# Distance attention: the position products written to PSUM in one row without gaps, and ACT's copies reading them with a stride

## The chip, the cores and the metric

The kernel runs on one core of a Trainium2 chip. The metric is the device time of one execution in microseconds (us). The times given for the kernel before are those of three executions, with their median.

## The reference

The model is a chain of layers over x of shape (8, 512, 128), all float32: a wave attention, a mixture of experts, a distance attention, and the same mixture of experts again, each after a layer norm and added to x. Only the distance attention is touched:

```python
# B = 8, S = 512, 16 heads of 8 dims, hidden 128
q = (x @ Wq.T + bq).reshape(B, S, HEADS, HEAD_DIM)      # k and v alike
scores = jnp.einsum('bqhd,bkhd->bhqk', q, k) / math.sqrt(HEAD_DIM)
pos_emb = dist_emb[MAX_POS - 1 + distance]              # distance = pos_q - pos_k
scores = scores + jnp.einsum('bqhd,qkd->bhqk', q, pos_emb)
scores = scores + jnp.einsum('bkhd,qkd->bhqk', k, pos_emb)
probs = jax.nn.softmax(scores, axis=-1)
ctx = jnp.einsum('bhqk,bkhd->bqhd', probs, v)
```

The second and the third line of scores are the two parts that the change is about: for a query position and a key position both take the same row of a table of distances, once against q and once against k.

## The kernel before, in words

**Sizes.** P = 128 is a tile of positions, QT = 4 tiles make the 512 positions, BH = 32 is the number of (batch, head) pairs worked at a time (two batches of 16 heads). The float32 operands are split into bfloat16 parts beforehand, 48 rows of them, and laid at rows 0 and 64 of a tile, so that a product reads 112 rows.

**Units and groups.** The function `distance_attention` walks NU = 64 units. A unit u is one pair of a query tile q and a key tile kt for 32 heads, with q, kt = divmod(u, 4). Four units (kt = 0 to 3) make a group, that is one query tile against all keys; there are 16 groups. In the text a unit is named by its kt, and "unit 0 of the next group" follows unit 3.

**Steps of a unit.** The order on TensorE (PE) is written out by hand in `unit_steps` and `plan`:

- "r", eight times (CH = 8): `positions` (L1690) computes the position products of 16 places for 32 heads, for the query part and the key part (s = 2) at once. It issues 8 products (HALF = 8). Each takes one slice of the table T, 128 columns wide, as its weights, and one pair of places of qk as the data that moves: 2 parts x 2 places x 32 heads = 128 columns. The 8 products fill a slot of psR (two PSUM banks of 512 float32). ACT's `keep` (L1772) copies the slot to r in SBUF, where a head's 128 places lie together. r has one buffer, so the first copy of a unit waits for VectorE (DVE) to have finished with the unit before.
- "c", four times: `content` (L1707) computes q times k for 8 heads (L1714) and adds to it the query part turned by a transpose of r (L1717). DVE's `add` (L1807, the instruction is L1814) adds the key part and writes S. Content begins when ACT has done all eight copies.
- With the fourth unit of a group S is complete. Then, during unit 0 of the next group, DVE takes the maxima and subtracts them (`maximum`, L1822 to L1829), PE turns S ("e", `turn`, L1726), ACT takes the exponential (`weigh`, L1786), PE multiplies with the values ("pv", `values`, L1742), ACT copies the result (L1794) and PE turns it ("o", L1751). In that unit six of the eight r steps stand ahead of the first e, the other two after e steps 1 and 3, and the four c steps near the end.

All steps but pv take a slot of psR in turn. There are RING = 3 slots, so a step waits until the step three before it has been read.

**What feeds a unit.** SP loads the parts of k for unit u (`load_k`, L1615) once the content of unit u - 2 is done. POOL (GpSimd) then spreads them to qk (`spread_k`, two copies at L1653), and the first r step of the unit waits for that. After the spread of unit 2 of a group POOL also spreads the next group's q (`spread_q`, two copies more), ahead of the spread of unit 3.

**The lines of the change.** In `positions` the output of a product is a view in which a part's 32 heads are 8 elements apart and its 2 places lie side by side:

```python
out = slot[:, 2 * j // HALF, :].rearrange("p (s h n) -> p s n h", s=2, h=BH)
mm = pe.matmul(out[:, :, n:n + 2, :], T[:, w:w + P], qk[...], start=(n == 0), stop=True, ...)
```

The product writes it in the order part, place, head, so that each of its 128 results goes 8 elements (32 bytes) behind the one before. The slot then holds, per bank, 64 (part, head) pairs with 8 places side by side, and ACT reads each bank from end to end, writing to r in runs of 8.

**Elsewhere**, a line that the rows name: in the wave output DVE's L977 reads from PSUM one column of each 32, four bytes every 128 bytes.

Of the kernel before, what the change touches and what calls it, by code (L numbers as in the profile page):

```python
# [15 lines left out]
P = 128  # L16
# [1494 lines left out]
def distance_attention(nc, sb, ps, sem, a, X, ident, dram):  # L1511
# [8 lines left out]
    BH = NB * H  # L1520
# [4 lines left out]
    CP = P // CH  # L1525
    HALF = CP // 2
    HB = BH // 4
    NPAIR = BH // 2
    RING = 3
# [35 lines left out]
    with ExitStack() as c:  # L1565
        T = sb(c, "T", [ROWS, WIN], BF16)
        qs = sb(c, "qs", [ROWS, 2, BH, P], BF16)
        ks = sb(c, "ks", [ROWS, 2, BH, P], BF16)
        qk = sb(c, "qk", [ROWS, 4, PAIRS, 2, BH], BF16)
        r = sb(c, "r", [P, 2, BH, P])  # L1570
# [4 lines left out]
        m = sb(c, "m", [P, BH])  # L1575
# [3 lines left out]
        psR = ps(c, "psR", [P, RING, 2, L])  # L1579
# [11 lines left out]
        act_took = sem(c, "act_took")  # L1591
# [86 lines left out]
        @block.tensor  # L1678
        def _(pe):

            def free_slot(n):
                if n >= RING:
                    old = fills[n - RING]
                    if old in by_act:
                        pe.wait_ge(act_took, by_act[old])
                    else:
                        pe.wait_ge(dve_took, by_dve[old])
                return psR[:, n % RING, :, :]

            def positions(u, k):  # L1690
                q, kt = divmod(u, QT)
                mine, theirs = q % 2, 2 + u % 2
                w0 = L - 1 + P * (kt - q % QT) - (P - 1)
                if k == 0:
                    pe.wait_ge(qb_ready, 2 * (q + 1))
                    pe.wait_ge(kb_ready, 2 * (u + 1))
                slot = free_slot(fill["r", u, k])
                for j in range(HALF):
                    pair = k * HALF + j
                    w, n = w0 + 2 * pair, 2 * j % HALF  # L1700
                    out = slot[:, 2 * j // HALF, :].rearrange("p (s h n) -> p s n h", s=2, h=BH)
                    mm = pe.matmul(out[:, :, n:n + 2, :], T[:, w:w + P],  # L1702
                                   qk[:, mine:theirs + 1:theirs - mine, pair, :, :], start=(n == 0), stop=True,
                                   skip_group_check=True)
                mm.then_inc(filled, 1)

            def content(u, k):  # L1707
                q = u // QT
                if k == 0:
                    pe.wait_ge(act_took, by_act["r", u, CH - 1])  # L1710
                slot = free_slot(fill["c", u, k]).rearrange("p a (h n) -> p (a h) n", n=P)
                for j in range(HB):
                    h = k * HB + j
                    pe.matmul(slot[:, j, :], qs[:, q % 2, h, :], ks[:, u % 2, h, :], start=(j % HG == 0),  # L1714
                              stop=False, skip_group_check=True)
                for j in range(HB):
                    mm = pe.matmul(slot[:, j, :], r[:, 0, k * HB + j, :], ident[:], start=False, stop=True,  # L1717
                                   is_transpose=True, skip_group_check=True)
                mm.then_inc(filled, 1)

            def turn(q, j):
                pe.wait_ge(shifted, q * BH + 2 * j + 2)
                slot = free_slot(fill["e", q, j])
                for i in range(2):
                    for kt in range(QT):
                        mm = pe.matmul(slot[:, i, kt * P:(kt + 1) * P], S[:, 2 * j + i, kt * P:(kt + 1) * P],  # L1726
                                       ident[:], start=(kt == 0), stop=True, is_transpose=True,
                                       skip_group_check=True)
                mm.then_inc(filled, 1)

            def values(q, j):
                i, g = divmod(j, GPB)
                pe.wait_ge(act_took, by_act["e", q, 2 * j + 1])
                if g == 0:
                    if i == 0:
                        pe.wait_ge(v_loaded, 16 * NB * (q // QT + 1))
                    if q:
                        pe.wait_ge(o_taken, (q - 1) * NB + i + 1)
                for kt in range(QT):
                    for h in range(HG):  # L1740
                        row, pair = h * (P // HG), q * NPAIR + 2 * j + h // 2
                        mm = pe.matmul(psO[row:row + VW, i, g, :], Vb[:, i, g, kt, h, :],  # L1742
                                       W[:, pair % RING_W, h % 2, kt * P:(kt + 1) * P],
                                       start=(kt == 0), stop=(kt == QT - 1), skip_group_check=True)
                mm.then_inc(pv, 1)

            def outputs(q, i):
                pe.wait_ge(o_taken, q * NB + i + 1)
                slot = free_slot(fill["o", q, i])
                for g in range(GPB):  # L1750
                    mm = pe.transpose(slot[:, 0, g * P:(g + 1) * P], oS[:, g * P:(g + 1) * P], ident[:])  # L1751
                mm.then_inc(filled, 1)

            pe.wait_ge(t_loaded, 32)
            pe.wait_ge(zeroed, 2)
            pe.wait_ge(psO_clear, 1)
            for kind, i, k in plan:
                if kind == "r":
                    positions(i, k)
                elif kind == "c":  # L1760
                    content(i, k)
                elif kind == "e":
                    turn(i, k)
                elif kind == "pv":
                    values(i, k)
                else:
                    outputs(i, k)

        @block.scalar
        def _(act):  # L1770

            def keep(u, k):  # L1772
                n = fill["r", u, k]
                act.wait_ge(filled, n + 1)
                if u:
                    act.wait_ge(dve_took, by_dve["c", u - 1, 3])
                act.copy(r[:, :, :, k * CP:(k + 1) * CP].rearrange("p s h (a n) -> p a (s h) n", a=2),  # L1777
                         psR[:, n % RING, :, :].rearrange("p a (m n) -> p a m n", n=HALF)).then_inc(act_took, 1)

            def weigh(q, j):  # L1780
                n = fill["e", q, j]
                act.wait_ge(filled, n + 1)
                pair = q * NPAIR + j
                if pair >= RING_W:
                    act.wait_ge(pv, (pair - RING_W) // 2 + 1)
                act.activation(W[:, pair % RING_W, :, :].rearrange("p a n -> p (a n)"),  # L1786
                               psR[:, n % RING, :, :].rearrange("p a n -> p (a n)"),
                               ACT.Exp, scale=1.0 / SHARP).then_inc(act_took, 1)

            def take(q, i):  # L1790
                if q or i:
                    act.wait_ge(filled, fill["o", q - (i == 0), 1 - i] + 1)
                act.wait_ge(pv, q * NQUAD + (i + 1) * GPB)
                act.copy(oS[:].rearrange("p (g n) -> p g n", g=GPB), psO[:, i, :, ::-1]).then_inc(o_taken, 1)  # L1794

            for kind, i, k in plan:
                if kind == "r":
                    keep(i, k)
                elif kind == "e":
                    weigh(i, k)  # L1800
                elif kind == "pv" and k % GPB == GPB - 1:
                    take(i, k // GPB)
# [107 lines left out]
```

## Time and profile before

| | |
|---|---|
| three executions | 4349.21, 4342.15, 4345.97 us, median 4345.97 us |
| the profiled execution | 4344.16 us, its span 4342.3 us |
| mean granted TensorE clock | 0.927 |
| busy over the span | PE 83%, DVE 78%, ACT 66%, PE weight load 52%, POOL 29% |
| distance attention | about 2636 us to 3988 us of the span |

The span is the time from the first to the last instruction of the profiled execution; the 1.9 us beside it lie outside. PE is TensorE's matmuls, PEld its weight loads. A matmul's end is modelled, and matmuls overlap one another: a run of matmuls is read by the time of the whole run and their number. The granted clock is a share of TensorE's full speed of 2.4 GHz; its other level is 1.2 GHz, shown as 0.5, and a stretch in between has had both.

### The profile page before, as it was taken

The page shows a single profiled execution, that of the slowest core. Times are in us where ns is not written, and L with a number is a line of the kernel's source. Part 1 is how long each engine was busy: PE and PEld are TensorE (multiplying, and loading weights), DVE is VectorE, ACT ScalarE, POOL GpSimd, SP SyncE. Part 2 cuts the span into 40 slices and gives each one's busy share as a digit, 9 for nine tenths or more (in the row PEclk, how much of TensorE's full clock was granted, in tenths as well). Part 3 has the DMA queues.
Part 4 walks back from the last instruction along what each step waited for, and adds up shares of the span by engine and source line. Part 5 has one row for each costly group of instructions (what it writes and reads, how often), then busy time and mean ns, then how long its engine had stood idle before and what let it go on. Part 6 is the DMA issues. An engine that isn't in the chain of part 4 may idle for free. (4 is left out here: it accounts for less than half of the span.)

```text
span 4342.3 us, 63839 instructions
## 1 busy us (share of the span) xinstructions
PE 3591.7 (83%) x22996; PEld 2264.5 (52%) x22996; DVE 3403.1 (78%) x4519; ACT 2865.8 (66%) x2433; POOL 1257.6 (29%) x918
## 2 busy tenths in 40 slices
PE   4899999999999999998479436989898898887891
PEld 2333333333333333333359425888888888887690
DVE  6999999999999999999475445677766766776662
ACT  3999999999999999998033133555555555554430
POOL 1121111221122111221014416354445435431245
PEclk7899999999999999999679768999999999998895
DMA  5000000000000000000222264223222222312022
GB/s 148 7 12 12 9 9 12 12 12 6 12 12 12 12 6 12 12 12 5 102 69 59 54 139 85 39 51 61 41 45 58 52 43 53 59 31 70 27 65 66
DMA packets 149517, 173.94 MB, mean 40 GB/s; under 512 B 63768, under 2 KB 124744, under 8 KB 141104
## 3 DMA queue, kind: packets, MB, share of 16 engines
q1 hardware_dynamic: 140592, 153.02, 15.4%
q0 software_dynamic: 8704, 17.84, 1.8%
q8 instruction: 154, 2.52, 0.3%
q14 instruction: 67, 0.55, 0.1%
HBM read 118.81 MB, written 52.00 MB: 39 GB/s over the span
## 5 line engine op out<-in xcount | busy, mean ns | idle before, releaser
L704 PE MATMUL psA<-wave,diag 128*128 128x512 f32 x3072 | 1432.7, 617 | 137.6 <-DVE score L860 88.9
L772 ACT ACTIVATE wave<-wave 128x2048 f32<-128x2048 int32 x640 | 1180.8, 1904 | 2.5 <-DVE wave L847 1.5
L704 PEld LDWEIGHTS psA<-wave,diag 128*128 128x128 f32 x3072 | 579.5, 195 | 891.9 <-issue 692.3
L1777 ACT COPY r<-psR 128x1024 f32<-128x1024 f32 x512 | 481.0, 1045 | 444.5 <-PE psR L1702 251.1
L641 POOL TENSOR_TENSOR diag<-ident,par 128x128 f32<-128x128 f32 x384 | 295.6, 797 | 1433.0 <-PE psA L704 1433.0
L1653 POOL COPY qk<-ks 48x2048 bf16<-48x2048 bf16 x128 | 482.1, 3766 | 717.9 <-DMA ks<-kb_parts 647.1
L822 DVE TENSOR_SCALAR wave<-s,par 128x2048 int32<-128x2048 int32 x480 | 611.3, 1274 | 0.0
L847 DVE TENSOR_SCALAR wave<-wave 128x2048 int32<-128x2048 int32 x512 | 608.6, 1213 | 0.0
L1814 DVE TENSOR_TENSOR S<-psR,r 128x1024 f32<-128x1024 f32 x256 | 313.5, 1225 | 373.2 <-PE psR L1717 355.1
L1702 PE MATMUL psR<-qk,T 112*128 112x128 bf16 x4096 | 469.7, 314 | 63.6 <-POOL qk L1653 45.5
L1702 PEld LDWEIGHTS psR<-qk,T 112*128 112x128 bf16 x4096 | 435.7, 136 | 87.5 <-issue 74.0
L737 ACT ACTIVATE s<-psS,par 128x1024 int32<-128x1024 f32 x256 | 282.8, 1105 | 126.9 <-PE psS L667 126.9
L1786 ACT ACTIVATE W<-psR 128x1024 f32<-128x1024 f32 x256 | 251.8, 1040 | 142.6 <-PE psR L1726 142.6
L860 DVE SCALAR_TENSOR_TENSOR score<-wave,par,psA 128x1024 f32<-128x1024 f32 x256 | 317.4, 1270 | 34.3 <-PE psA L704 34.3
L860 DVE SCALAR_TENSOR_TENSOR score<-wave,par,score 128x1024 f32<-128x1024 f32 x256 | 316.3, 1273 | 0.0
L1829 DVE TENSOR_SCALAR S<-S,m 128x512 f32<-128x512 f32 x512 | 309.9, 677 | 2.3
L1726 PE MATMUL psR<-ident,S 128*128 128x128 f32 x2048 | 261.1, 282 | 48.4 <-DVE S L1829 47.1
L1822 DVE TENSOR_REDUCE mx<-S 128x8 f32<-128x1024 f32 x256 | 297.8, 1211 | 0.0
L1726 PEld LDWEIGHTS psR<-ident,S 128*128 128x128 f32 x2048 | 229.8, 144 | 75.4 <-DVE S L1829 61.1
L1717 PE MATMUL psR<-ident,r 128*128 128x128 f32 x2048 | 266.9, 273 | 0.0
L754 ACT ACTIVATE score<-score 128x2048 f32<-128x2048 f32 x132 | 241.4, 1899 | 6.1 <-DVE score L860 5.7
L679 PE MATMUL psO<-score,Vg 128*9 128x512 f32 x1056 | 238.1, 593 | 7.0 <-ACT score L754 7.0
(252 smaller groups left out, 3981.0 us busy)
## 6 DMA issues: line engine op xcount, KB each, us to landing
ks<-kb_parts SPq DMA_DIRECT2D x128, 384.0 KB, 6.0
qs<-qb_parts SPq DMA_DIRECT2D x32, 384.0 KB, 8.8
ys<-f_ys SPq DMA_DIRECT2D x36, 256.0 KB
wave_out<-og SPq DMA_DIRECT2D x33, 256.0 KB, 2.1
o<-wave_out SPq DMA_DIRECT2D x8, 1024.0 KB, 5.3
qp<-qa_parts SPq DMA_DIRECT2D x32, 192.0 KB, 3.5
kp<-ka_parts SPq DMA_DIRECT2D x32, 192.0 KB, 4.0
f_wu<-in_w_up SPq DMA_DIRECT2D x2, 2048.0 KB, 9.5
```

Source lines behind the costliest of these rows:

```text
L704: mm = pe.matmul(psA[:, kt, :], diag[:, h % 2, f, :], wave[:, h % 2, f, kt * L:(kt + 1) * L], start=(f == 0), stop=(f == PE_F - 1), skip_g ...
L772: act.activation(wave[:, h % 2, f, :], angle[:, h % 2, f, :], ACT.Sin, scale=float(TWO_PI / 2.0 ** 32)).then_inc(sine, 1)
L822: dve.tensor_scalar(angle[:, h % 2, f, :], src, scalar, par[:, u, row, h * NF + f:h * NF + f + 1], ALU.mult, ALU.add).then_inc(turned if f ...
L847: dve.tensor_scalar(angle[:, h % 2, f - 1, :], at, 32 - FRAC, None, ALU.logical_shift_left).then_inc(cut, 1)
L860: dve.scalar_tensor_tensor(out=score[:, u * HG + h, cols], in0=wave[:, h % 2, f, cols], scalar=par[:, u, 1, h * NF + f:h * NF + f + 1], in ...
L1653: pool.tensor_copy(dst[rows, :, odd, :], src[rows, :, :].rearrange("r h (n two) -> r n h two", two=2)[:, :, :, odd]).then_inc(ready, 1)
L1702: mm = pe.matmul(out[:, :, n:n + 2, :], T[:, w:w + P], qk[:, mine:theirs + 1:theirs - mine, pair, :, :], start=(n == 0), stop=True, skip_g ...
L1726: mm = pe.matmul(slot[:, i, kt * P:(kt + 1) * P], S[:, 2 * j + i, kt * P:(kt + 1) * P], ident[:], start=(kt == 0), stop=True, is_transpose ...
L1777: act.copy(r[:, :, :, k * CP:(k + 1) * CP].rearrange("p s h (a n) -> p a (s h) n", a=2), psR[:, n % RING, :, :].rearrange("p a (m n) -> p ...
L1814: dve.tensor_tensor(S[:, hs, kt * P:(kt + 1) * P], psR[:, n % RING, :, :].rearrange("p a (h n) -> p (a h) n", n=P), r[:, 1, hs, :], ALU.ad ...
L1822: dve.tensor_reduce(mx[:, hs, kt], S[:, hs, kt * P:(kt + 1) * P], AX.X, ALU.max).then_inc(maxed, 1)
L1829: dve.tensor_scalar(S[:, h, :], S[:, h, :], m[:, h:h + 1], None, ALU.subtract).then_inc(shifted, 1)
```

## The change

The 8 products of an r step write their 128 results side by side, in the order place, part, head (n, s, h), four products to a bank. The data that moves is read in that order too: 32 heads, then the other part, then the other place. The weights, the products and their number are the same. ACT's copy delivers the same r: it now takes for each of the 64 (part, head) pairs its 16 places, which lie 64 elements (256 bytes) apart and over both banks, and writes them as one run of 16.

```diff
@@ positions @@
-                    w, n = w0 + 2 * pair, 2 * j % HALF
-                    out = slot[:, 2 * j // HALF, :].rearrange("p (s h n) -> p s n h", s=2, h=BH)
-                    mm = pe.matmul(out[:, :, n:n + 2, :], T[:, w:w + P],
-                                   qk[:, mine:theirs + 1:theirs - mine, pair, :, :], start=(n == 0), stop=True,
-                                   skip_group_check=True)
+                    w, bank, at = w0 + 2 * pair, j // (HALF // 2), j % (HALF // 2)
+                    mm = pe.matmul(slot[:, bank, at * P:(at + 1) * P].rearrange("p (n s h) -> p n s h", s=2, h=BH),
+                                   T[:, w:w + P],
+                                   qk[:, mine:theirs + 1:theirs - mine, pair, :, :].rearrange("r s n h -> r n s h"),
+                                   start=(at == 0), stop=True, skip_group_check=True)
@@ keep @@
-                act.copy(r[:, :, :, k * CP:(k + 1) * CP].rearrange("p s h (a n) -> p a (s h) n", a=2),
-                         psR[:, n % RING, :, :].rearrange("p a (m n) -> p a m n", n=HALF)).then_inc(act_took, 1)
+                act.copy(r[:, :, :, k * CP:(k + 1) * CP].rearrange("p s h n -> p (s h) n"),
+                         psR[:, n % RING, :, :].rearrange("p a (n m) -> p m (a n)", m=2 * BH)).then_inc(act_took, 1)
```

No wait, no buffer, no order of steps, no DMA and no instruction of POOL or DVE is changed.

## Rows read from the trace of the kernel before

**Rows 1.** Busy time by engine over the distance attention

```profile
core 0: us, PE busy (x) PEld busy (x) DVE busy (x) ACT busy (x) POOL busy (x), PEclk, DMA share, GB/s
...
2636.00:3988.00 1352.00, 1211.82 (x14464) 1111.55 (x14464) 949.42 (x1184) 744.69 (x801) 586.64 (x157) 0.99 0.25 48
```

**Rows 2.** Tile psR, its instructions: ns shortest/median/longest, first and last start

```profile
L1702 PE MATMUL psR<-qk,T x4096: 269/314/502, 2636.5 to 3949.3; 112*128 112x128 bf16 x196
...
L1714 PE MATMUL psR<-ks,qs x2048: 217/219/230, 2647.9 to 3955.7; 112*128 112x128 bf16 x187
...
L1777 ACT COPY r<-psR x512: 1012/1042/1095, 2638.4 to 3950.1; 128x1024 f32<-128x1024 f32 x171
```

**Rows 3.** Timeline of one group, PE: start us, us, operation; three units in order

```profile
2988.86 7.33 PE L1702 MATMUL psR<-qk,T 112*128 112x128 bf16 x64
...
3001.99 1.04 PE L1717 MATMUL psR<-ident,r 128*128 128x128 f32 x8
3003.19 7.15 PE L1702 MATMUL psR<-qk,T 112*128 112x128 bf16 x64 [0.16 <-issue]
...
3016.30 1.04 PE L1717 MATMUL psR<-ident,r 128*128 128x128 f32 x8
```

**Rows 4.** Timeline of unit 3 of that group and the next start, all engines

```profile
3018.41 7.15 PE L1702 MATMUL psR<-qk,T 112*128 112x128 bf16 x64 [1.07 <-issue]
...
3019.48 7.43 ACT L1777 COPY r<-psR 128x1024 f32<-128x1024 f32 x8 [7.67 <-PE psR L1702]
...
3026.96 0.62 PE L1714 MATMUL psR<-ks,qs 112*128 112x128 bf16 x8 [1.41 <-ACT r L1777]
...
3032.28 4.00 PE L1702 MATMUL psR<-qk,T 112*128 112x128 bf16 x35
...
3033.79 2.84 ACT L1777 COPY r<-psR 128x1024 f32<-128x1024 f32 x3 [6.89 <-DVE S L1814]
```

**Rows 5.** Timeline of POOL over the same group

```profile
2995.53 7.57 POOL L1653 COPY qk<-ks 48x2048 bf16<-48x2048 bf16 x2 [33.24 <-DMA ks<-kb_parts]
3003.15 7.49 POOL L1653 COPY qk<-qs 48x2048 bf16<-48x2048 bf16 x2
3010.70 7.61 POOL L1653 COPY qk<-ks 48x2048 bf16<-48x2048 bf16 x2
3024.06 7.54 POOL L1653 COPY qk<-ks 48x2048 bf16<-48x2048 bf16 x2 [5.75 <-DMA ks<-kb_parts]
```

**Rows 6.** Timeline of PE from 3018.41, cut behind the second and the third product

```profile
3018.41 0.38 PE L1702 MATMUL psR<-qk,T 112*128 112x128 bf16 x2 [1.07 <-issue]
...
3018.41 0.49 PE L1702 MATMUL psR<-qk,T 112*128 112x128 bf16 x3 [1.07 <-issue]
```

**Rows 7.** DVE lines L977, L1348 and L1814, reading PSUM: ns shortest/median/longest

```profile
L977 DVE TENSOR_SCALAR orec<-psG x8: 223/224/226, 2087.5 to 2138.6; 128x64 f32<-128x64 f32 x8
...
L1348 DVE TENSOR_SCALAR f_h<-f_pp x144: 680/691/693, 2292.6 to 4242.1; 128x512 f32<-128x512 f32 x144
...
L1814 DVE TENSOR_TENSOR S<-psR,r x256: 1223/1225/1226, 2649.5 to 3956.8; 128x1024 f32<-128x1024 f32 x128
```

**Rows 8.** Timeline of the very first unit of the attention, PE and ACT

```profile
2636.49 10.17 PE L1702 MATMUL psR<-qk,T 112*128 112x128 bf16 x64 [45.47 <-POOL qk L1653]
2638.39 1.01 ACT L1777 COPY r<-psR 128x1024 f32<-128x1024 f32 x1 [41.68 <-PE psR L1702]
...
2643.21 4.68 ACT L1777 COPY r<-psR 128x1024 f32<-128x1024 f32 x5 [0.39 <-PE psR L1702]
```

**Rows 9.** Timeline inside unit 0 of a group, where DVE subtracts the maxima

```profile
2954.61 7.67 POOL L1653 COPY qk<-ks 48x2048 bf16<-48x2048 bf16 x2 [7.57 <-DMA ks<-kb_parts]
2955.03 9.91 DVE L1829 TENSOR_SCALAR S<-S,m 128x512 f32<-128x512 f32 x8
...
2962.62 2.80 PE L1726 MATMUL psR<-ident,S 128*128 128x128 f32 x16 [2.91 <-DVE S L1829]
```

**Rows 10.** Stretches from unit 3's end to unit 0's, PE alone, with the granted clock

```profile
2864.80:2904.00 39.20, 36.27 (x518) 1.00 0.24 42
2947.70:2988.60 40.90, 37.99 (x519) 0.96 0.22 40
```

## The prediction

> **What bounds the kernel now.** I read the stretches first: the distance attention takes 1352 us, PE is busy for 1212 us of them, and nothing of the change lies outside [rows 1]. A busy PE is not a PE at its peak, so I looked at what a product costs. 64 position products in a row last 7.15 us and one alone 314 ns: (7.15 - 0.31)/63 = 109 ns from start to start [rows 2, 3]. Eight content products, also bfloat16, also 112 rows by 128 columns, last 0.62 us with 219 ns for one [rows 2, 4]: (0.62 - 0.22)/7 = 57 ns. The position products run at half the rate of the same product with a straight output.
>
> That is no loss yet, because ACT keeps the pace. Its eight copies of a unit last 7.43 us, (7.43 - 1.01)/7 = 0.917 us from one to the next, while PE makes a slot in 8 x 0.109 = 0.87 us [rows 2, 4]. ACT is thus never more than the first slot behind PE: in unit 3 of the group shown PE starts at 3018.41 and the first copy at 3019.48, 1.07 us later; the last copy ends at 3026.91 and content begins at 3026.96 [rows 4]. The path through a unit is first slot, eight copies, content.
>
> Last I asked what starts the next unit, by the starts of the r steps: unit 1 at 2988.86, 2 at 3003.19, 3 at 3018.41, 0 of the next group at 3032.28, so units of 14.33, 15.22 and 13.87 us [rows 3, 4]. PE's pauses ahead of units 2 and 3 are put down to "issue", and POOL's timeline tells what they are: its spread of k for unit 2 ends at 2995.53 + 7.57 = 3003.10, the one for unit 3 at 3010.70 + 7.61 = 3018.31, each 0.1 us before PE goes on [rows 3, 5]. The first waited for a DMA that SP issues at the end of unit 0's content; the second stands behind the spread of q (3003.15 to 3010.64), POOL busy all the while. Neither depends on how fast PE and ACT were in units 1 and 2. For unit 0 of the next group POOL is ready at 3031.60 and PE comes at 3032.28: there PE and ACT's path decides [rows 4, 5]. So of each group only unit 3 pays for a shorter first slot; in unit 0, ACT's first copy waits for DVE's last add of the unit before (1.51 us after PE's start, not 1.07), and behind that DVE decides, whose subtractions stand still while POOL spreads: 9.91 us for eight, and PE sits idle for 2.91 us [rows 4, 9].
>
> **The change part by part.** *The output without gaps.* I take 57 ns per product for 109. That it is the output that halves the rate, I read from the first starts: the second product starts 0.38 - 0.314 = 0.07 us after the first, the third 0.49 - 0.314 = 0.18 us [rows 2, 6]. PE takes in a product's 128 columns in some 60 ns when nothing is queued, and falls to 110 ns from the third on, as behind a full outlet. The first slot is then ready after 7 x 0.057 + 0.22 = 0.62 us instead of 7 x 0.109 + 0.314 - 0.045 = 1.03 us: 0.41 us earlier. The bound below is no gain (the weights or the reading were the cause), above nothing better than the content row.
>
> *The reading in runs of 32 instead of 64.* The same 128 columns and the same weights; cost nothing, and up to the whole gain if short runs were what costs.
>
> *ACT's copy with a stride of 256 bytes.* 1024 elements as before. The trace has no ACT read like it. Nearest is DVE's L977, which reads 64 float32 from PSUM that lie 128 bytes apart (one column of each 32) in 224 ns. L1348 reads 512 adjacent ones in 691 ns. Both L1348 and L1814 (1024 elements, 1225 ns) read straight, and between them lie (1225 - 691)/512 = 1.04 ns per element [rows 7]. A straight read of 64 would thus be expected at 691 - 448 x 1.04 = 225 ns; with the gaps it is 224. So the strided read costs DVE nothing, and I take nothing for ACT. Bound below: no gain, since the copies already read straight and 0.917 us for 1024 elements is ACT's pace for straight data too. Bound above: a doubling, as PE's writes have it [rows 2, 4]: 0.87 us per copy.
>
> Against the change speaks a rule of the Trainium skill (Vector Engine (DVE) Microarchitecture Reference, 5.2, the access granule): in SBUF a port of DVE keeps its rate only for runs of at least two adjacent 4-byte words, and a hop at every element costs it about 0.65 cycle. Carried over to ACT and PSUM that would be an estimate, by the page's 0.83 ns per element of ACT, of 0.65 x 0.83 x 1024 = 0.55 us per copy, and by the working of rival A some 4530 us instead of 4336.6. L977's 224 ns does not bear the rule out for DVE's reads of PSUM; of ACT's no row tells.
>
> *ACT's write in runs of 16 instead of 8:* nothing; it is part of the same 0.917 us.
>
> *The sum.* Unit 3 of each of the 16 groups: 16 x 0.41 = 6.6 us. Units 1 and 2 gain nothing (the work that hides it is POOL's spread); unit 0 nothing of its own: DVE's add and POOL's DMA both move with the end of unit 3. The very first unit is another case. TensorE is still at its lower level, 1.2 GHz, and PE needs 2638.39 - 2636.49 = 1.90 us for the first slot, and PE, not ACT, sets the pace for the first copies: they end at 2643.21 + 4.68 = 2647.89, 11.4 us after PE's start [rows 8]. At half the clock a straight product would take twice 57, 114 ns, a slot 0.91 us, which just keeps ACT's pace; ACT starts after some 1.15 us (7 x 0.114 and the way out) and ends 7.43 us later, at 8.6 us: 2.8 us gained, and all later units hang on it. Sum -9.4 us. On the profiled execution's 4344.16 us that gives 4334.8; the median lies 1.8 us above it, so 4336.6.
>
> *The clock.* The pause of 2.91 us in unit 0 [rows 9] is followed in some groups by a stretch at 1.2 GHz. I looked at that stage in the 15 groups that have it: 8 show a granted clock of 0.96 and 40.8 to 41.2 us, 7 show 1.00 and 39.1 to 39.5 us; one of each stands in [rows 10]. A dip costs 1.6 us. The pause grows by 0.4 us, since the last r step in it ends earlier. I leave the number of dips as it is, and put 3 more or fewer, 5 us, into the range.
>
> **The rivals.**
> *A: ACT's copies get slower.* With x us more per copy, unit 3 gets 8x longer against 0.41 gained, so from x = 0.05 us the groups lose. Units 1 and 2 have up to 14.33 - 13.87 = 0.46 and 15.22 - 13.87 = 1.35 us of cover, 1.8 together [rows 3, 4]; unit 0 the pause of 2.9 us. From x = 0.14 on (16 x (8x - 0.41) - 2.8 = 8.7) the kernel would be measurably slower. At half of the doubling, 0.44 us: units 1 and 2 together 2 x (3.5 - 0.4) - 1.8 = 4.4, unit 3 3.1, unit 0 3.5 - 2.9 = 0.6, so 8.1 x 16 = 130 us, less 2.8: 4473. At the doubling, 0.87 us: (11.3 + 6.5 + 4.1) x 16 = 350 us: 4690. For it: no ACT row excludes it; against it: L977. Chance 0.15, a fifth of that for an x so small that it only eats the gain.
> *B: the products don't get faster.* Then nothing moves: 4346. Against it: the first starts [rows 6]. Chance 0.07.
> *C: the clock.* PE, done sooner and waiting for ACT, is granted 1.2 GHz more often. The mild form: the longer pause brings a dip in nearly all groups, 7 x 1.6 = 11 us, which cancels the gain: 4347, chance 0.06. The grave form: the clock falls inside the r steps and content, 5.3 us at full speed [rows 4], takes up to twice as long: 5.3 for unit 3 and 2 x 5.3 - 1.8 for units 1 and 2, 14.1 x 16 = 226 us for all groups, 4560; in one to four groups 4350 to 4390. Against it: PE's idle of 1.4 us ahead of content leaves the clock alone. Chance 0.04.
>
> **How the numbers follow.** The forecast (faster products, unchanged copies, dips within 3 of today's) has chance 0.68, its own range 4329 to 4344. 0.2% is 8.7 us, about what a measurement of this kernel can tell from no change, so the line lies at 4337.3, just above 4336.6; fewer dips put it safely on the fast side, more put it within. I give 0.46 of the 0.68 to faster and 0.22 to the same. With B, the mild C and the small A the same has 0.38; slower has 0.16. The range of 4328 to 4372 holds the forecast, B, the mild C and the small A, some 0.8; the large A and most of the grave C are left out.
>
> **What would show it.** Position products 56 to 60 ns apart (a run of 64 still 7 us long, waiting for ACT); L1777's median within 10 ns of 1042; first copy 0.65 us after PE's start in unit 3, that unit 13.45 us; units 1 and 2 still 14.3 and 15.2 us, PE's pauses ahead of units 2 and 3 longer by 0.4 us; the first unit's copies ended 8.6 us after its start. A median of L1777 above 1100 ns would make the prediction wrong, as would a granted clock below 0.98 in the attention.

## The result, and the profile after

The changed kernel takes 4461.77 us in the median of four runs (4456.27 to 4465.69), the kernel before 4347.59 us in its four. The ratio is 1.0262, 95% interval 1.0244 to 1.028: 114 us slower. The profiled execution has a span of 4454.4 us. I had put a chance of 0.16 on slower.

The first view is the tile psR, each line's shortest, median and longest duration in ns.

```profile
L1701 PEld LDWEIGHTS psR<-qk,T x4096: 95/98/152, 2632.2 to 4059.2; 112*128 112x128 bf16 x196
L1701 PE MATMUL psR<-qk,T x4096: 217/219/314, 2632.2 to 4059.3; 112*128 112x128 bf16 x196
...
L1714 PE MATMUL psR<-ks,qs x2048: 217/264/314, 2640.8 to 4068.5; 112*128 112x128 bf16 x187
...
L1777 ACT COPY r<-psR x512: 1007/1045/1099, 2633.3 to 4060.2; 128x1024 f32<-128x1024 f32 x171
```

The position products (now L1701) went from a median of 314 to 219 ns, and ACT's copies stayed at 1042 to 1045 [rows 2]. Both things that the change does came out as forecast. But content, which the change does not touch, went from 219 to 264 ns. The stretches tell why; the third number from the end is the granted clock.

```profile
core 0: us, PE busy (x) PEld busy (x) DVE busy (x) ACT busy (x) POOL busy (x), PEclk, DMA share, GB/s
2826.20:2835.40 9.20, 5.45 (x74) 4.22 (x72) 6.21 (x8) 7.43 (x8) 2.92 (x1) 0.98 0.44 85
2835.40:2841.70 6.30, 6.30 (x59) 6.20 (x58) 3.59 (x3) 0.00 (x0) 6.18 (x3) 0.77 0.01 3
2841.70:2851.10 9.40, 5.18 (x74) 3.98 (x72) 5.82 (x6) 7.43 (x8) 8.08 (x3) 1.00 0.46 84
2851.10:2857.60 6.50, 6.50 (x60) 6.41 (x58) 3.54 (x3) 0.00 (x0) 5.21 (x2) 0.74 0.01 3
2857.60:2867.40 9.80, 6.57 (x74) 5.20 (x73) 5.87 (x6) 7.43 (x8) 2.62 (x1) 0.74 0.42 80
2867.40:2874.80 7.40, 7.40 (x60) 7.25 (x59) 3.63 (x3) 0.00 (x0) 4.74 (x2) 0.66 0.01 3
...
2636.00:4100.00 1464.00, 1225.03 (x14431) 1087.79 (x14428) 947.60 (x1182) 743.82 (x799) 578.11 (x155) 0.83 0.23 44
```

Over the distance attention the granted clock is 0.83, against 0.99 [rows 1], and it is not low everywhere. The rows are units 1, 2 and 3 of a group, each as its r steps and then its content: the r steps have 0.98, 1.00 and 0.74, the content behind them 0.77, 0.74 and 0.66. In the r steps the low clock costs ACT nothing: its eight copies are busy for the same 7.43 us in all three. In content it does cost. The timeline shows the first of these units, PE and ACT.

```profile
2826.17 0.61 PE L1701 MATMUL psR<-qk,T 112*128 112x128 bf16 x8
...
2827.22 1.72 PE L1701 MATMUL psR<-qk,T 112*128 112x128 bf16 x24 [0.43 <-DVE S L1814]
2827.25 7.43 ACT L1777 COPY r<-psR 128x1024 f32<-128x1024 f32 x8 [3.41 <-DVE S L1814]
...
2829.23 0.62 PE L1701 MATMUL psR<-qk,T 112*128 112x128 bf16 x8 [0.29 <-ACT r L1777]
...
2831.98 0.62 PE L1701 MATMUL psR<-qk,T 112*128 112x128 bf16 x8 [0.30 <-ACT r L1777]
...
2834.73 0.87 PE L1714 MATMUL psR<-ks,qs 112*128 112x128 bf16 x8 [2.13 <-ACT r L1777]
2835.40 1.91 PE L1717 MATMUL psR<-ident,r 128*128 128x128 f32 x8
2837.11 1.06 PE L1714 MATMUL psR<-ks,qs 112*128 112x128 bf16 x8
...
2839.48 1.04 PE L1717 MATMUL psR<-ident,r 128*128 128x128 f32 x8
```

ACT's eight copies last 7.43 us as before. PE, twice as fast, now has a wait of some 0.3 us ahead of most slots and one of 2.13 us ahead of content, where it had run through and then paused for 1.41 us [rows 4]. Eight transposes then take 1.91 us in place of the 1.04 that they take at full clock [rows 3], and only near the end of content are they back at 1.04. In this profile unit 3 of the groups lasts 17.1 us in the median, as much as unit 2; before it was 13.9 [rows 3, 4 show one].

### The profile page after: what moved, and what is told of

Its sections match the earlier page's. It is cut to its first block and busy times, and to the rows that moved or that the text cites. A ratio compares the mean times of both kernels' runs of the same rounds, so it can differ in the third digit from the quotient of the medians.

```text
span 4454.4 us, 63839 instructions
## 1 busy us (share of the span) xinstructions
PE 3603.9 (81%) x22996; PEld 2241.0 (50%) x22996; DVE 3399.5 (76%) x4519; ACT 2867.3 (64%) x2433; POOL 1254.2 (28%) x918
## 5 line engine op out<-in xcount | busy, mean ns | idle before, releaser
L1814 DVE TENSOR_TENSOR S<-psR,r 128x1024 f32<-128x1024 f32 x256 | 313.5, 1225 | 484.4 <-PE psR L1717 475.6
L1701 PE MATMUL psR<-qk,T 112*128 112x128 bf16 x4096 | 339.5, 236 | 146.7 <-ACT r L1777 72.9
L1701 PEld LDWEIGHTS psR<-qk,T 112*128 112x128 bf16 x4096 | 265.3, 105 | 213.8 <-ACT r L1777 119.1
L1786 ACT ACTIVATE W<-psR 128x1024 f32<-128x1024 f32 x256 | 251.8, 1024 | 154.1 <-PE psR L1726 153.9
L1717 PE MATMUL psR<-ident,r 128*128 128x128 f32 x2048 | 348.0, 327 | 0.0
L1726 PE MATMUL psR<-ident,S 128*128 128x128 f32 x2048 | 289.8, 302 | 44.5 <-DVE S L1829 43.2
L1726 PEld LDWEIGHTS psR<-ident,S 128*128 128x128 f32 x2048 | 261.1, 158 | 66.4 <-DVE S L1829 56.8
L1717 PEld LDWEIGHTS psR<-ident,r 128*128 128x128 f32 x2048 | 291.1, 173 | 0.0
L1714 PE MATMUL psR<-ks,qs 112*128 112x128 bf16 x2048 | 212.5, 266 | 93.2 <-ACT r L1777 93.2
```

What stands on the lines that cost most here:

```text
L1701: mm = pe.matmul(slot[:, bank, at * P:(at + 1) * P].rearrange("p (n s h) -> p n s h", s=2, h=BH), T[:, w:w + P], qk[:, mine:theirs + 1:the ...
L1814: dve.tensor_tensor(S[:, hs, kt * P:(kt + 1) * P], psR[:, n % RING, :, :].rearrange("p a (h n) -> p (a h) n", n=P), r[:, 1, hs, :], ALU.ad ...
```

## The experiments

Beside the first four experiments the kernel before had a median of 4342.89 us, beside the later seven one of 4322.8 or 4321.58 us. So I compare ratios between the two sets, not times.

**1. Only ACT's stride.** Before, with the changed copy. The places in r come out in another order.

```diff
-                act.copy(r[...].rearrange("p s h (a n) -> p a (s h) n", a=2),
-                         psR[...].rearrange("p a (m n) -> p a m n", n=HALF))
+                act.copy(r[...].rearrange("p s h n -> p (s h) n"),
+                         psR[...].rearrange("p a (n m) -> p m (a n)", m=2 * BH))
```

> The products of before, with their gaps; only ACT's copy reads with the stride of 256 bytes. The places in r come out in another order, so the attention's values are not the reference's; the work is the same. Theory 1 (the loss comes from the granted clock, which falls because PE now waits between its r steps and ahead of content; the strided read is free): L1777's median stays 1042 to 1050 ns, granted clock in the attention 0.98 to 0.99, time that of before, 4340 to 4356. Theory 2 (the strided read costs, by being slower or by disturbing PE's writes and content): 4360 to 4460, or a lower clock as in the changed kernel.

Measured: 4345.52 us, ratio 1.0003 (0.9993 to 1.0013). The source line of the copies:

```profile
L1777 ACT COPY r<-psR x512: 1012/1042/1095, 2642.7 to 3956.2; 128x1024 f32<-128x1024 f32 x171
```

Reading 1024 float32 in steps of 256 bytes takes ACT the same 1042 ns as reading them straight. Theory 2, and my rival A, are out.

**2. Only the products.** The changed products with the straight copy of before; the places in r are in another order again.

```diff
-                act.copy(r[...].rearrange("p s h n -> p (s h) n"),
-                         psR[...].rearrange("p a (n m) -> p m (a n)", m=2 * BH))
+                act.copy(r[...].rearrange("p s h (a n) -> p a (s h) n", a=2),
+                         psR[...].rearrange("p a (m n) -> p a m n", n=HALF))
```

> The products without gaps of the changed kernel; ACT's copy reads straight, as before. The places in r come out in another order, so the attention's values are not the reference's. Theory 1: the whole loss stays, 4450 to 4475, products 56 ns apart, granted clock in the attention about 0.83. Theory 2: the loss goes with the stride, 4335 to 4360.

Measured: 4458.16 us, ratio 1.0267 (1.025 to 1.0284): all of the loss. The stretch of the attention:

```profile
2636.00:4100.00 1464.00, 1225.34 (x14301) 1089.06 (x14302) 945.17 (x1178) 741.25 (x795) 581.85 (x156) 0.82 0.22 44
```

**3. The products twice over.** The changed kernel, every r step's eight products issued twice.

```diff
-                for j in range(HALF):
+                for j in [*range(HALF), *range(HALF)]:
...
-                                   start=(at == 0), stop=True, skip_group_check=True)
+                                   start=True, stop=True, skip_group_check=True)
```

> The changed kernel, but each r step issues its eight products twice over, the second time onto the first's results, so that PE is busy 0.9 us per slot as it was with the gaps. Theory 1: the clock comes back, 0.97 to 0.99 in the attention, content's transposes are 109 ns apart again, and the time is that of before, 4338 to 4358, though PE does 4096 products more. If what PE does in the r steps is not what lowers the clock, or the layout itself costs: 4440 to 4480.

Measured: 4347.15 us, ratio 1.0011 (1.0 to 1.0023). The stretch of the attention, and a unit's end and the next one's start on PE:

```profile
2636.00:3988.00 1352.00, 1218.67 (x18460) 1140.62 (x18458) 948.39 (x1181) 741.89 (x798) 585.93 (x156) 0.98 0.25 48
```

```profile
3011.41 0.62 PE L1714 MATMUL psR<-ks,qs 112*128 112x128 bf16 x8 [1.27 <-ACT r L1777]
3011.86 1.04 PE L1717 MATMUL psR<-ident,r 128*128 128x128 f32 x8
...
3018.14 7.31 PE L1701 MATMUL psR<-qk,T 112*128 112x128 bf16 x128 [1.26 <-issue]
```

4096 products that do nothing useful take the 114 us away again, to within 0.2%: clock 0.98, transposes 1.04 us for eight. The layout itself costs nothing; the loss comes of PE having too little to do in the r steps, by way of the clock.

**4. Only the first slot.** In the first r step of a unit the products and the copy are the changed ones, in the other seven those of before.

```diff
                 for j in range(HALF):
                     pair = k * HALF + j
+                    if k == 0:
+                        w, bank, at = w0 + 2 * pair, j // (HALF // 2), j % (HALF // 2)
+                        mm = pe.matmul(slot[:, bank, at * P:(at + 1) * P].rearrange("p (n s h) -> p n s h", s=2, h=BH),
+                                       T[:, w:w + P], qk[...].rearrange("r s n h -> r n s h"), start=(at == 0), ...)
+                        continue
...
+                if k == 0:
+                    act.copy(r[...].rearrange("p s h n -> p (s h) n"),
+                             psR[...].rearrange("p a (n m) -> p m (a n)", m=2 * BH))
+                    return
```

> Only the first r step of each unit has products without gaps (and its copy the stride); the other seven are as before. My forecast's term: the first slot of unit 3 comes 0.41 us sooner, 16 times, and something in the very first unit, while PE stays busy for the rest: Theory 1 expects the clock of before and 4336 to 4346, the unit 3 of a group 13.45 us. If even one r step in eight with a pause behind it lowers the clock: 4360 or more.

Measured: 4343.11 us, ratio 0.9999 (0.9988 to 1.0011). The clock of the attention is 0.98. The gain that I forecast is not seen in the time. Experiment 8 is the cleaner look at it.

**5. Half with gaps.** Of a slot's eight products four without and four with gaps; half of the places in r are in another order.

```diff
+                    if j < HALF // 2:
                         w, bank, at = w0 + 2 * pair, j // (HALF // 2), j % (HALF // 2)
...
+                        continue
+                    w, n = w0 + 2 * pair, 2 * j % HALF
+                    out = slot[:, 2 * j // HALF, :].rearrange("p (s h n) -> p s n h", s=2, h=BH)
+                    mm = pe.matmul(out[:, :, n:n + 2, :], T[:, w:w + P], qk[...], start=(n == 0), ...)
```

> Of a slot's eight products four are without gaps and four with; PE is then busy about 0.66 us per slot of ACT's 0.92, against 0.87 before and 0.45 in the changed kernel. The copy reads with the stride, so half of the places in r are in another order and the attention's values are not the reference's. If the loss grows in step with PE's waiting: granted clock in the attention about 0.90 and 4390 to 4420. If the clock falls only beyond some amount of waiting: either that of before (4338 to 4352, clock 0.98) or that of the changed kernel (4450 to 4470). I lean to the first end of the last two, since before's own 1.4 us pause did nothing.

**6. Twice in the last r step alone.** The waits between the steps stay, the pause ahead of content is made shorter.

```diff
-                for j in range(HALF):
+                for j in [*range(HALF if k == CH - 1 else 0), *range(HALF)]:
```

> The changed kernel, with the eight products of the last r step of a unit alone issued twice: PE's pause ahead of content falls from 2.1 to about 1.7 us, the short waits between the r steps stay. If it is the long pause that lowers the clock: 4345 to 4390. If it is the waits between the r steps: still 4440 to 4465.

**7. Twice in all but the last.** The waits are filled, the long pause stays.

```diff
-                for j in range(HALF):
+                for j in [*range(HALF if k < CH - 1 else 0), *range(HALF)]:
```

> The changed kernel with the products of all r steps but the unit's last issued twice: the waits between the r steps are gone, the pause of 2.1 us ahead of content stays. If the waits between the steps lower the clock: 4338 to 4365. If the pause does: 4430 to 4465.

Measured: experiment 5 has a ratio of 1.0057 (1.0038 to 1.0076), 6 of 1.0037 (1.0019 to 1.0056), 7 of 1.0046 (1.0032 to 1.006). The stretches of the attention in that order:

```profile
2636.00:3988.00 1352.00, 1167.13 (x14020) 998.45 (x14024) 931.88 (x1160) 720.06 (x777) 576.11 (x154) 0.95 0.24 46
```

```profile
2636.00:3988.00 1352.00, 1098.06 (x14731) 964.41 (x14732) 946.98 (x1178) 729.92 (x789) 576.82 (x155) 0.96 0.25 48
```

```profile
2636.00:3988.00 1352.00, 1196.97 (x17583) 1118.46 (x17581) 932.96 (x1149) 725.38 (x780) 579.20 (x154) 0.96 0.25 48
```

And waits of PE in experiments 5, 6 and 7 (total us, times, longest), one fence each:

```profile
PE psR L1702 <- ACT r L1784: 7.8, 30, 0.3
```

```profile
PE psR L1701 <- ACT r L1777: 87.6, 270, 0.5
PE psR L1714 <- ACT r L1777: 79.1, 47, 1.7
```

```profile
PE psR L1714 <- ACT r L1777: 86.5, 47, 2.1
```

I had asked which of the two lowers the clock, the short waits or the long pause. The answer is neither alone: with 270 short waits and a pause of at most 1.7 us, or with a pause of up to 2.1 us and no short waits that the list names, the clock stands at 0.96 and the kernel loses 0.4 to 0.5%; with both it stands at 0.83 and the kernel loses 2.6%. My lean in experiment 5, the clock of before, was also off: halving the products' saving gives 0.95 and 0.6%. The loss is more with both than with the two added. The profiles show how. Of the 48 contents in units 1 to 3, none is slowed in the kernel before and all 48 are in the changed kernel, with 8.3 us from first product to last transpose in the median instead of 5.5; in experiments 5, 6 and 7 it is 22, 27 and 15 of them, and the slowest takes 7.1 us. Experiment 5 also says that the list of waits is a poor measure: it names 30 short waits for ACT, 7.8 us in all, and the clock is no higher than with the 270 of experiment 6.

**8. Twice in all but the first r step.** The forecast's term by itself: first slot sooner, PE kept busy behind it.

```diff
-                for j in range(HALF):
+                for j in [*range(HALF if k else 0), *range(HALF)]:
```

> The changed kernel with the products of all r steps but the unit's first issued twice: PE is as busy as before from the second slot on and has the first 0.41 us sooner. If the clock holds (0.98), this is what my forecast priced: unit 3 13.5 us, 4 to 10 us less than before, ratio 0.998 to 0.999. If the first slot's shorter work lowers the clock now and then, as it may have in the kernel where only the first slot was changed: ratio 1.000 to 1.003.

Measured: ratio 0.9989 (0.9975 to 1.0003). Timeline of unit 3 of a group, PE and ACT:

```profile
3002.08 6.86 PE L1701 MATMUL psR<-qk,T 112*128 112x128 bf16 x120 [1.81 <-issue]
...
3002.73 7.43 ACT L1777 COPY r<-psR 128x1024 f32<-128x1024 f32 x8 [7.99 <-PE psR L1701]
...
3015.53 4.64 PE L1701 MATMUL psR<-qk,T 112*128 112x128 bf16 x73
```

The first copy comes 0.65 us after PE's start and unit 3 is 13.45 us long (3015.53 - 3002.08), both to the hundredth as forecast. By the ratio the time is some 5 us less, with an interval from 11 less to 1 more, so that this run does not tell it from no change. The very first unit gains little here: its extra products hold PE up while the clock is still low.

**9. Pairs.** The products write in the order part, head, place: two float32 side by side, then six left out. ACT reads straight.

```diff
-                    out = slot[:, 2 * j // HALF, :].rearrange("p (s h n) -> p s n h", s=2, h=BH)
-                    mm = pe.matmul(out[:, :, n:n + 2, :], T[:, w:w + P],
-                                   qk[:, mine:theirs + 1:theirs - mine, pair, :, :], ...)
+                    out = slot[:, 2 * j // HALF, :].rearrange("p (s h n) -> p s h n", s=2, h=BH)
+                    mm = pe.matmul(out[:, :, :, n:n + 2], T[:, w:w + P],
+                                   qk[:, ..., pair, :, :].rearrange("r s n h -> r s h n"), ...)
```

> The layout in PSUM and ACT's straight copy of before, but the product writes in the order part, head, place: runs of two float32 side by side, then a gap of six; the data that moves is read one element at a time. If gaps between pairs are free for PE's writes (the skill's rule on PSUM has pairs as what counts) and the reading is too: products 56 ns apart and, by the clock, the loss of the changed kernel, ratio 1.020 to 1.030. If the writes in pairs still halve the rate, or the reading does: 109 ns and ratio 0.998 to 1.002. Above 109 ns both would add up, and PE would set the pace: ratio over 1.03.

Measured: ratio 1.01 (1.0082 to 1.0118), none of the three expectations. One unit's products in the timeline, and the stretches of the content ahead of them and of these r steps:

```profile
3008.10 8.05 PE L1702 MATMUL psR<-qk,T 112*128 112x128 bf16 x64
```

```profile
3001.00:3008.00 7.00, 6.74 (x64) 6.66 (x65) 3.48 (x3) 0.20 (x1) 6.88 (x3) 0.76 0.00 1
3008.00:3016.00 8.00, 8.00 (x67) 6.26 (x65) 5.93 (x6) 6.38 (x7) 7.21 (x3) 1.00 0.53 99
```

The products are (8.05 - 0.29)/63 = 123 ns apart, slower than with the gaps of before. The start of the attention tells which side sets that pace, for there all three kernels run at 1.2 GHz. The first unit's products, here in pairs, and then 2 us at a granted clock of 0.50, PE alone, of the kernel before, of the changed kernel and of this one:

```profile
2626.22 8.05 PE L1702 MATMUL psR<-qk,T 112*128 112x128 bf16 x64 [45.58 <-POOL qk L1653]
```

```profile
2638.50:2640.50 2.00, 2.00 (x12) 0.50 0.00 0
```

```profile
2634.20:2636.20 2.00, 2.00 (x22) 0.50 0.00 0
```

```profile
2628.20:2630.20 2.00, 2.00 (x19) 0.50 0.00 0
```

With the gaps of before 12 products touch these 2 us (213 ns from start to start), without gaps 22 (107 ns), in pairs 19 (123 ns). The first two take twice their time at full clock; the pairs take 8.05 us for 64 here too, most of them at 1.2 GHz. So writing in pairs does not halve the rate as a gap behind every element does, and what holds these products at 123 ns does not follow TensorE's clock. That leaves the reading one element at a time, the other thing that this kernel changes, though no run changes it alone.

By its rows PE is busy without a wait in the r steps, and its pause ahead of content is 1.10 us, shorter than in the kernel before. Yet the content shown has a clock of 0.76, and 22 of the 48 are slowed. Waits and pauses that a profile shows are thus not all that the clock answers to.

**10. POOL's spread of q behind that of unit 3's k.** The kernel before, with this alone changed.

```diff
                 spread_k(u)
-                if u % QT == 2 and u // QT + 1 < NQ:
+                if u % QT == 3 and u // QT + 1 < NQ:
                     spread_q(u // QT + 1)
```

> The kernel before, but POOL spreads the next group's q after unit 3's k and not ahead of it. My reading that POOL alone sets the start of unit 3, 1.1 us after PE is ready: unit 2 shrinks from 15.2 to about 14.3 us, 16 times, so 8 to 18 us less, 4326 to 4336, if the clock holds. If the pause is something else, or unit 0's k now comes later by the same: no change, 4338 to 4350.

Measured: ratio 0.9945 (0.9925 to 0.9964), 4303.1 us against 4322.8: 20 us less by the medians, 16 to 32 by the interval, a little more than the 8 to 18 expected. POOL's timeline over a group, ACT's, and the starts of units 3 and 0 on PE:

```profile
2980.05 7.57 POOL L1653 COPY qk<-ks 48x2048 bf16<-48x2048 bf16 x2 [34.41 <-DMA ks<-kb_parts]
2994.08 7.55 POOL L1653 COPY qk<-ks 48x2048 bf16<-48x2048 bf16 x2 [6.46 <-DMA ks<-kb_parts]
3001.70 7.48 POOL L1653 COPY qk<-qs 48x2048 bf16<-48x2048 bf16 x2
3009.23 7.58 POOL L1653 COPY qk<-ks 48x2048 bf16<-48x2048 bf16 x2
```

```profile
2988.96 7.43 ACT L1777 COPY r<-psR 128x1024 f32<-128x1024 f32 x8 [6.89 <-DVE S L1814]
3003.27 7.43 ACT L1777 COPY r<-psR 128x1024 f32<-128x1024 f32 x8 [6.89 <-DVE S L1814]
```

```profile
3001.76 7.29 PE L1702 MATMUL psR<-qk,T 112*128 112x128 bf16 x64
...
3016.91 5.40 PE L1702 MATMUL psR<-qk,T 112*128 112x128 bf16 x48 [0.67 <-issue]
```

Unit 3's k is ready at 3001.63 and its copies start 14.31 us after unit 2's, where it was 15.10 (3019.48 [rows 4] less 3004.38, where the same timeline has unit 2's first copy). ACT's wait for unit 3 is now for DVE's last add.

But this is not where the gain lies. POOL's work was not made less, only moved: its spread for unit 0 now ends at 3009.23 + 7.58 = 3016.81, and PE starts unit 0 0.1 us later. By the starts in the two profiles the median unit 2 is 0.8 us shorter (14.4 for 15.2) and the median unit 3 is 1.3 us longer (15.2 for 13.9). Unit 0 is some 1.0 us shorter in the mean of 15 (39.6 for 40.6): ACT's first copy comes 1.07 us after PE's start, no longer 1.51, and PE's longest pause is 2.3 us in the median, no longer 3.0. From first product to last content the attention takes 1310.1 us, before 1320.3. So the profiles place 10 us of the gain; the rest they do not, as the one profile of the kernel before is from the earlier set. Why PE's pause in unit 0 got shorter was not tried.

**11. Both.** Experiments 8 and 10 together.

```diff
-                for j in range(HALF):
+                for j in [*range(HALF if k else 0), *range(HALF)]:
...
-                if u % QT == 2 and u // QT + 1 < NQ:
+                if u % QT == 3 and u // QT + 1 < NQ:
```

> The products without gaps, issued twice in all r steps but the first, together with POOL's later spread of q. With POOL out of the way PE starts unit 3 as soon as content of unit 2 is done, and ACT's first copy waits for DVE's last add (1.5 us after PE's start) whatever PE does. So the first slot should bring nothing more: ratio 0.993 to 0.996, that of the later spread alone. If DVE were not what ACT waits for: 0.990 to 0.992.

Measured: ratio 0.9958 (0.9945 to 0.9971), within the interval of experiment 10. The products without gaps add nothing that can be seen to the better order on POOL. Beside the reason given ahead of the run there is a second: POOL sets the end of unit 3 as well. In the same place its spread for unit 0 ends at 3017.45 and PE starts at 3017.55, and unit 3 lasts 15.3 us in every group. Both this and experiment 10 beat the two kernels; experiment 10, the old products with POOL's later spread, does it without products that do nothing.

## Why the prediction was wrong, point by point

- **What a product costs** was right: 219 ns in the median, 56 apart, the content row's values.
- **That the strided read costs ACT nothing** was right, 1042 ns in experiment 1. DVE's L977 had been a fair stand-in, and the granule rule of the Trainium skill (Vector Engine (DVE) Microarchitecture Reference, 5.2), stated for SBUF, did not carry over to ACT's reads of PSUM.
- **The step that failed is the clock**, in "the change part by part" and in rival C. I priced only the pause in unit 0 (2.91 us, 0.4 us longer) and left the clock everywhere else as it was, on the ground that 1.4 us of idle ahead of content did no harm. But the change makes that pause up to 2.1 us and adds a wait of some 0.3 us ahead of most slots. My list of signs had PE "waiting for ACT" in the r steps, but no term of the sum gave that waiting a price. I had the numbers for it: PE makes a slot in 0.45 us and ACT takes one per 0.917 us, and what is left over is a wait. Experiments 2 and 3 show what it costs: the products alone bring all of the loss (1.0267), and with PE filled up again it is gone (1.0011). The row with a clock of 0.99 told of a PE that had no such waits [rows 1], and I read it as if it told of the change too.
- **How the loss is made up.** In the changed kernel's profile the content of units 1 to 3 takes 8.3 us in the median instead of 5.5, from first product to last transpose. By the medians of the starts in the two traces units 1, 2 and 3 have grown by 2.4, 1.9 and 3.2 us, 7.5 together. From the first product to the last content the attention takes 1437.4 us against 1320.3, 117 longer, of which the span shows 112. Rival C's grave form had the place right and, with 226 us for a clock at 1.2 GHz through all of content, the size twice too large: content is at the lower level for about half of its work (5.5 us of it became 8.3, not 11). The mistake was its chance of 0.04. The mild form came true beside it: 13 of the 15 units 0 behind a group now last 41.0 to 41.3 us, where 7 of them had taken 39.5 to 39.9; in the mean they grew by 0.4 us, 6 us in all.
- **Why the first slot brings nothing there.** With POOL no longer last, PE starts a unit's first slot as content of the unit before ends, and ACT's first copy waits for DVE (1.5 us after PE's start in units 2 and 3). I had seen this for unit 0 and did not ask what it does when other units take longer.
- **The gain of 9.4 us.** Experiment 8 shows unit 3's part at its place, 13.45 us, and a total of 1 more to 11 less; experiment 4 shows no gain. The first unit's part was right in the changed kernel: its copies end 8.5 us after PE's start, against 11.4 [rows 8]; half of it was lost again in the content behind, for the whole unit lasts 15.3 us against 16.8.
- **That POOL sets the start of units 2 and 3** was right for unit 3 by experiment 10, where POOL then sets the start of unit 0 in its place.

What is shown is that the loss is the clock's, and that what PE does in the r steps decides it. What stays open is which property of PE's work the clock answers to: experiment 9 had it fall without a wait in the r steps, and PE's busy time in the rows does not tell it. It was not tried which of its two edits, the writing in pairs or the reading in single elements, does that.

## What to carry to other kernels

A faster product on an engine that waits for another engine does not shorten the path; it turns work into waits, and TensorE's clock can answer with its lower level just where PE is the bound. So before making PE faster, work out PE's time per slot against the pace of whoever empties it, and count the waits as well as the longest pause: here either alone cost 0.4 to 0.5%, both together 2.6%. It is a warning sign, not a measure, as experiment 9 lost 1% with no such wait and a shorter pause. If the clock falls, repeating products is a quick test, and the gain, if any, lies in what the chain of starts waits for: here the order of two spreads on POOL was worth 0.5%. Look then at where it came from: the wait that was to go had moved one unit on, and the time was saved in another.

## What the runs showed of the hardware

- A bfloat16 product of 128 columns whose results go to PSUM 32 bytes apart takes 109 ns from start to start at full clock, against 56 without gaps. At 1.2 GHz it is 213 against 107 ns; the first slot with the gaps took 1.90 us there, against 1.07 at full clock [rows 8, 4]. The change reads the moving data in another order as well (runs of 32, not 64), and no run varied that alone; the content products, with straight output, have the same 57 ns [rows 2, 4].
- Results in pairs of float32 with gaps behind them, the moving data read one element at a time: 123 ns at 2.4 GHz and at 1.2 GHz alike (experiment 9). At 1.2 GHz that is well below the 213 ns of a gap behind every element.
- Products with gaps, 109 ns apart and without a wait between the slots, left the attention at a granted clock of 0.99 [rows 1]; products without gaps, with waits between the slots and ahead of content, at 0.83; those of experiment 9, 123 ns apart and again without a wait between the slots, at 0.94:

```profile
2636.00:3988.00 1352.00, 1259.98 (x14001) 1086.89 (x13999) 927.85 (x1137) 735.42 (x775) 577.23 (x154) 0.94 0.25 47
```

- ACT reads float32 from PSUM 256 bytes apart, over two banks, at its straight pace: 1042 ns for 1024.
